# A two-layer attention kernel: its order of work rebuilt in beats of two head pairs

## The reference, cut to what matters

```
x: (64, 128, 160)   ctx: (64, 77, 256)          # 64 batch rows
# layer 0, 20 heads of 64
n = layer_norm(x);  x = x + attention(n, n)      # self, keys 128
n = layer_norm(x);  x = x + attention(n, ctx)    # cross, keys 77
h = layer_norm(x) @ w1 + b1;  a, gate = split(h) # 160 -> 2 * 640
x = x + (a * gelu(gate)) @ w2 + b2
# layer 1, 20 heads of 8
q = x @ W_q;  text keys/values from ctx[:, :73], image keys/values from ctx[:, 73:]
probs_t = softmax(q k_t / sqrt(8));  text_out = probs_t v_t
qsem = l2norm(probs_t @ ctx_text);  sem = qsem . l2norm(ctx_ip)
probs_ip = softmax(q k_ip / sqrt(8) + 0.5 sem) * spatial_mask
out = (text_out + probs_ip v_ip) @ W_out + b_out + x
```

## Time and profile before

| | |
|---|---|
| median of two runs | 3803.65 us |
| span of the profiled execution | 3799.1 us |
| TensorE busy | 3608.9 us, 95% |
| VectorE busy | 2547.7 us, 67% |
| ScalarE busy | 2592.4 us, 68% |
| GpSimd busy | 1352.4 us, 36% |
| mean granted TensorE clock | 0.995 |

### The profile page before, as it was taken

How to read it: one execution, slowest core, us unless ns; L and a number is a source line. 1 busy time by engine, 2 the same in 40 slices (tenths; PEclk the granted TensorE clock), 3 DMA queues, 4 the chain that set the end, 5 groups by cost and what they waited for, 6 DMA issues and landing times.

```text
span 3799.1 us, 88944 instructions
## 1 busy us (share of the span) xinstructions
PE 3608.9 (95%) x29708; PEld 3328.8 (88%) x29708; DVE 2547.7 (67%) x8159; ACT 2592.4 (68%) x8021; POOL 1352.4 (36%) x1658
## 2 busy tenths in 40 slices
PE   6999999999999999999999999999999999999997
PEld 5888989889898898988989899898988989889897
DVE  6667666676766666676676766767667676666766
ACT  6667676766767667676676766767676676766764
POOL 2233343333433334333333433334333343333433
PEclk9999999999999999999999999999999999999998
DMA  6522314223142321413223132231422313232130
GB/s 169 163 64 75 103 44 119 60 85 91 41 122 58 96 77 51 123 47 106 70 60 117 45 112 65 76 103 44 121 57 87 90 41 121 58 96 77 53 93 18
DMA packets 210716, 313.38 MB, mean 82 GB/s; under 512 B 31232, under 2 KB 167520, under 8 KB 210272
## 3 DMA queue, kind: packets, MB, share of 16 engines
q1 hardware_dynamic: 209984, 307.53, 27.6%
q10 hardware_dynamic: 288, 0.16, 0.0%
HBM read 267.97 MB, written 14.42 MB: 74 GB/s over the span
## 4 chain that ended last, share of the span: by engine, by line
PE 60%; DVE 17%; ACT 11%; issue 8%; POOL 4%; DMA 1%; SPq 0%; ACTq 0%; DVEq 0%; POOLq 0%
PE PS L818 8%; PE PT L840 6%; PE PV L854 6%; PE PW L798 5%; PE PG L659 5%; ACT SE L989 4%; PE PG L651 4%; PE PG L634 4%; PE PV L864 3%; DVE sums L1233 3%; PE PG L637 3%; PE PG L635 3%; PE PG L636 3%; POOL SE L1404 3%; PE PG L742 2%
## 5 line engine op out<-in xcount | busy, mean ns | idle before, releaser
L1404 POOL TENSOR_TENSOR SE<-SE,rs 128x512 f32<-128x512 f32 (+1 forms) x640 | 557.6, 871 | 1761.8 <-DVE rs L1238 1761.8
L989 ACT ACTIVATE SE<-PS,mx 128x128 f32<-128x128 f32 (+2 forms) x3840 | 982.6, 346 | 240.7 <-DVE qq L1262 128.5
L975 ACT ACTIVATE PTs<-PT 128x512 f32<-128x512 f32 (+2 forms) x960 | 575.4, 599 | 87.1 <-PE PT L840 67.9
L840 PE MATMUL PT<-ident,SE 128*128 128x128 f32 (+2 forms) x3840 | 582.0, 274 | 36.4 <-POOL SE L1404 34.6
L1233 DVE TENSOR_REDUCE sums<-SE 128x4 f32<-128x512 f32 (+1 forms) x640 | 367.0, 573 | 337.8 <-ACT SE L989 336.9
L1222 DVE TENSOR_REDUCE mx<-PS 128x4 f32<-128x512 f32 (+2 forms) x960 | 504.4, 525 | 72.1 <-PE PS L818 58.7
L840 PEld LDWEIGHTS PT<-ident,SE 128*128 128x128 f32 (+2 forms) x3840 | 465.5, 144 | 64.5 <-POOL SE L1404 49.0
L1396 POOL TENSOR_TENSOR n<-qq,p_half 128x4 f32<-128x4 f32 x320 | 345.3, 1079 | 490.2 <-DVE qq L1262 490.1
L798 PE MATMUL PW<-w_o,OTs 128*128 128x160 f32 x2560 | 415.3, 299 | 1.1 <-ACT OTs L967 1.1
L818 PE MATMUL PS<-qk 128*128 128x256 f32 x1280 | 348.5, 395 | 47.6 <-ACT qk L915 47.6
L912 ACT ACTIVATE qk<-PG 128x256 f32<-128x256 f32 x640 | 252.9, 395 | 190.1 <-PE PG L637 186.5
(11 more groups left out here) (207 smaller groups left out, 7828.5 us busy)
## 6 DMA issues: line engine op xcount, KB each, us to landing
q_slice<-q_split SPq DMA_DIRECT2D x630, 192.0 KB, 2.4
vc_slice<-vc_split SPq DMA_DIRECT2D x155, 512.0 KB, 3.6
kc_slice<-kc_split SPq DMA_DIRECT2D x150, 256.0 KB, 2.7
q1st<-q_hi SPq DMA_DIRECT2D x320, 32.0 KB, 1.9
k1st<-k_hi SPq DMA_DIRECT2D x160, 38.5 KB, 1.9
xres<-in_x_dram SPq DMA_DIRECT2D x32, 160.0 KB, 2.3
q1st<-q_lo SPq DMA_DIRECT2D x160, 32.0 KB, 1.9
out_dram<-x SPq DMA_DIRECT2D x64, 80.0 KB, 1.6
```

The costliest lines, as they stand in the source:

```text
L840: last = tr(PT[0:J, 128 * i:128 * i + 128], SE[:, place % 4, J * i:J * i + J], ident[:, :])
L975: a_(PTs[0:J, place % 3, :], PT[0:J, :], ACT.Copy).then_inc(S["pts_done"], 1)
L989: last = a_(SE[:, place % 4, J * i:J * i + J], PS[place % 2][:, step * i:step * i + J], ACT.Exp, bias=mx[:, place % 2, i:i + 1])
L1404: gp.tensor_tensor(e, e, rs[:, n % 2, :].unsqueeze(2).to_broadcast([128, 4, J]), ALU.mult)\
```

## The change

The slots are grouped in beats of three, 20 beats a group, and the unit of layer 0 becomes the duo: two head pairs (units 2d and 2d + 1). In a beat the queues hold:

- slot 0: scores of duo beat + 1, transposes of duo beat, products of duo beat - 1, the qk job of the first unit of duo beat + 2
- slot 1: the second qk job, the job "v", transposes and then scores of one unit of layer 1, and single jobs
- slot 2: single jobs, then the output projection of duo beat - 1 (both units), then the product of the unit of layer 1

Scores are four matmuls a unit instead of two: each reads 64 rows, one head, and the two heads go to the two banks of PS. Their weights and keys are the halves of qk without the zeros. Transposes are eight of 64 rows a unit instead of four of 128, the two row halves into the two banks of PT. Maximum, PT copy and OT copy are one instruction a duo. PS, PT and PV hold one duo each (before, two units in PS and in PV), and layer 1 shares PT and PV, with probabilities in tiles of its own (SE1, PTs1). The qk copy is one instruction, with the scale put into the weights' splits. The keys of cross attention are one VectorE copy into kx. x1 and cT get two sets. The norm's statistics stand in slot t, norm_out in t + 2 and xT in t + 3. The ff jobs stand in slots 51, 52, 53, 53, 54 and 66, 67, 68, 68, 69 instead of five in 56 and five in 68. keep_busy is gone.

```diff
-    STEP = 60
-    L1_SLOT = [6, 7, 9, 10, 11, 13, 14, 15, 17, 18, 22, 26, 27, 29, 33, 36, 38, 45, 49, 53]
-    NORM_SLOT = {(0, 0): -12, (0, 1): -2, (1, 0): 25, (1, 1): 40, (2, 0): 52, (2, 1): 65, (3, 0): 60, (3, 1): 71}
-    FF_SLOT = [56, 56, 56, 56, 56, 68, 68, 68, 68, 68]
+    BEATS = 20
+    STEP = 3 * BEATS
+    DUOS = NL0 // 2
+    NORM_SLOT = {(0, 0): -16, (0, 1): -1, (1, 0): 17, (1, 1): 32, (2, 0): 47, (2, 1): 62, (3, 0): 56, (3, 1): 71}
+    FF_SLOT = [51, 52, 53, 53, 54, 66, 67, 68, 68, 69]
+    DOWN_SLOT = [55, 70]
...
+                def scores(g, d):
+                    q = DUOS * g + d
+                    J, h = K0[2 * d // U0], 2 * d // NP % 2
+                    if q > 0:
+                        pe.wait_ge(S["exp_done"], 2 * q)
+                    for n in (2 * d, 2 * d + 1):
...
                         for b in range(HB):
+                            for e in range(2):
+                                rows, at = slice(DH * e, DH * e + DH), J * (2 * (n % 2) + b)
+                                last = mm(PS[:, e, at:at + J], qk[rows, n % 2, 0, 128 * b:128 * b + 128],
+                                          keys[rows, J * b:J * b + J], start=True, stop=True)
...
+                def probs_transposed(g, d):
+                    q, J = DUOS * g + d, K0[2 * d // U0]
+                    if q > 0:
+                        pe.wait_ge(S["pts_done"], q)
+                    if scored1[0]:
+                        pe.wait_ge(S["exp1_done"], scored1[0])
+                    if turned1[0]:
+                        pe.wait_ge(S["pts1_done"], turned1[0])
+                    for n in (2 * d, 2 * d + 1):
                         pe.wait_ge(S["p_done"], NL0 * g + n + 1)
+                        for i in range(4):
+                            for r in range(2):
+                                rows, at = slice(64 * r, 64 * r + 64), 64 * (4 * (n % 2) + i)
+                                last = tr(PT[0:J, r, at:at + 64], SE[rows, n % 4, J * i:J * i + J], ident[rows, rows])
```

TensorE's queue, slot by slot:

```diff
                 for t in range(FIRST, LAST):
+                    beat, part = divmod(t, 3)
+                    if part == 0:
+                        if duo_at(beat + 1):
+                            scores(*duo_at(beat + 1))
+                        if duo_at(beat):
+                            probs_transposed(*duo_at(beat))
+                        if duo_at(beat - 1):
+                            probs_v(*duo_at(beat - 1))
                     for name in qk_at(t):
                         job(name)
...
+                    if part == 1 and l1_at(beat - 1):
+                        probs_transposed1(*l1_at(beat - 1), turned)
+                    if part == 1 and l1_at(beat):
+                        scores1(*l1_at(beat), turned)
                     for name in late_at(t):
                         if name[0] != "v":
                             job(name)
+                    if part == 2 and duo_at(beat - 1):
+                        wo(g, 2 * d)
+                        wo(g, 2 * d + 1)
+                    if part == 2 and l1_at(beat - 1):
+                        probs_v1(*l1_at(beat - 1), multiplied)
```

ScalarE's queue:

```diff
+                    if sub == 0 and l1_at(beat - 1):
+                        exp1(*l1_at(beat - 1))
+                    if sub == 0 and duo_at(beat):
+                        pt_out(*duo_at(beat))
+                    if sub < 2 and duo_at(beat + 1):
+                        exp(g, 2 * d + sub)
                     for name in qk_at(t):
                         job(name)
+                    if sub == 0 and duo_at(beat - 1):
+                        ot_out(*duo_at(beat - 1))
+                    if sub == 1 and l1_at(beat - 1):
+                        pt1_out(*l1_at(beat - 1))
```

VectorE's queue, behind softmax_in in slot 0 and prob_sums(2d), "kc" and "v" in slot 1:

```diff
+                    if sub == 1 and duo_at(beat + 1):
+                        prob_sums(g, 2 * d + 1)
+                    if sub == 2 and l1_at(beat):
+                        softmax1_in(*l1_at(beat))
+                    if sub == 2 and l1_at(beat - 1):
+                        unit_out(*l1_at(beat - 1))
...
-                    for g, k, h in norms_at(t - 1):
+                    for g, k, h in norms_at(t - 2):
                         if k < 3:
                             norm_out(g, k, h)
```

More of the change, by code:

```diff
@@ L404, in xattn_program @@
                            for g in range(GROUPS) for h in range(2) for w in range(W1)]
-                          + [(STEP * g + K1_SLOT[1] + 1 + w, ("k1", g, 1, w)) for g in range(GROUPS) for w in range(W1)])
+                          + [(STEP * g + K1_STACK + w, ("k1", g, 1, w)) for g in range(GROUPS) for w in range(W1)])
         late_at = slots(
-            [(t, ("v", u[1], u[2] // 2)) for t, u in UNIT_AT.items() if u[0] == "l0" and u[2] % 2 == 0]
-            + [(t + (1 if k == 3 else 2), ("xT", g, k, h)) for t, g, k, h in NORMS]
@@ L416, in xattn_program @@
             + [(STEP * g + K1_SLOT[r], ("k1", g, r)) for g in range(GROUPS) for r in range(2)]
             + [(STEP * g + VIP_SLOT, ("vip", g, 0)) for g in range(GROUPS)]
-            + [(ctx1_slot(g, b), ("ctx1", g, b)) for g in range(GROUPS) for b in range(GB)])
+            + [(STEP * g + CTX1_SLOT[b], ("ctx1", g, b)) for g in range(GROUPS) for b in range(GB)])
         def qk_at(t):
-            if l0_at(t + 2) is None:
+            duo = duo_at(t // 3 + 2)
+            if t % 3 == 2 or duo is None:
@@ L422, in qk_at @@
                 return []
-            g, n = l0_at(t + 2)[1:]
+            g, n = duo[0], 2 * duo[1] + t % 3
             return [("qk", g, n)] + ([("kc", g, n - U0)] if U0 <= n < U0 + NP else [])
@@ new lines, in probs_v @@
+                def probs_v(g, d):
+                    q, J = DUOS * g + d, K0[2 * d // U0]
+                    pe.wait_ge(S["pts_done"], q + 1)
+                    pe.wait_ge(S["v_done"], q + 1)
+                    if q > 0:
+                        pe.wait_ge(S["ots_done"], q)
+                    if product1[0]:
+                        pe.wait_ge(S["on_done"], product1[0])
+                    for u in range(2):
+                        for b in range(HB):
+                            for e in range(2):
+                                at = 128 * (2 * e + b)
+                                last = mm(PV[DH * e:DH * e + DH, HT * u + 128 * b:HT * u + 128 * b + 128],
+                                          v_sb[0:J, d % 2, b, 2 * u + e, :], PTs[0:J, q % 2, u, at:at + 128],
+                                          start=True, stop=True)
+                    last.then_inc(S["pv_done"], 1)
@@ new lines, in probs_v1 @@
+                def probs_v1(g, k, multiplied):
+                    b, w, j = k // W1, k % W1, l1_count(g, k)
+                    pe.wait_ge(S["pts1_done"], j)
+                    if multiplied:
+                        pe.wait_ge(S["ots_done"], multiplied)
+                    if j > 1:
+                        pe.wait_ge(S["on_done"], j - 1)
+                    if w == 0:
+                        pe.wait_ge(S["gv_done"], NTH[("ctx1", g, b)])
+                        pe.wait_ge(S["gram_done"], NTH[("ctx1", g, b)])
+                    for i in range(4):
+                        off = D1 * (i % 2)
+                        last = mm(PV[:, GV * i + off:GV * i + off + GS + D1], PTs1[0:TT, 128 * i:128 * i + 128],
+                                  gv[:, b % 2, 2 * w + i // 2, off:off + GS + D1], start=True, stop=True)
+                    last.then_inc(S["pv1_done"], 1)
+                    product1[0] = j
@@ new lines, in exp1 @@
+                def exp1(g, k):
+                    j = l1_count(g, k)
+                    act.wait_ge(S["mx1_done"], j)
+                    act.wait_ge(S["sip_in"], j)
+                    if j > 2:
+                        act.wait_ge(S["qq_done"], j - 2)
+                    for i in range(4):
+                        last = a_(SE1[:, j % 2, TT * i:TT * i + TT], PT[:, 1, T * i:T * i + TT], ACT.Exp,
+                                  bias=mx1[:, j % 2, i:i + 1])
+                    last.then_inc(S["exp1_done"], 1)
@@ L997, in context_squares @@
                         act.wait_ge(S["c_dve"], HB * (2 * g + h))
+                    if g > 0:
+                        for w in range(W1):
+                            act.wait_ge(S[f"k1_in{w}"], 16 * 3 * g)
                     for b in range(HB):
```

501 lines of the change are left out of this document (216 added, 285 removed).

## The result

The changed kernel takes 4837.26 us (median of two runs, 4829.09 and 4845.43) against 3803.65, 1.271 times as long, with a 95% interval of 1.2685 to 1.274. The forecast was 3853, in a range of 3620 to 4080: 984 us too low, with the result outside its range.

A forecast was written before the change was run, and what follows sets the result against it. TensorE's queue was taken to bound the kernel, busy 95% of the span. Head 240, 15 groups of 233.9 (work -11.8, waits +14.2), tail 100 and 4.6 around the span gave 3853 us, range 3620 to 4080.

The forecast's parts named there:

- TensorE's work: Scores, transposes and changes of tile in a group: -8.4 - 1.6 - 3.2 + 1.4 = -11.8 us.
- rival 2: Scores and half transposes of every beat: row halves do not run side by side; 4190 us, chance 0.15.
- self transposes: Probabilities' transposes in self units: 128-column loads keep four paired steps at 0.11 us, so nothing saved.
- the middle: TensorE's added waits a group, taken between 0 and the net 28.3 us: 14.2 us.
- full price: All TensorE waits of the new order in a group: 36.6 us, or 28.3 net of today's 8.3 idle.
- xT: Transposes in the third slot wait for norm_out: 7.8 us a group in self beats, 3.5 in cross beats.
- GELU beats: Table loads and gelus lengthen ScalarE's loop to 16.0 us; TensorE loses 3.6 and 1.0, twice: 9.2 a group.
- norm_stats ahead of the maximum: VectorE's statistics delay the next maximum, which has 0.3 us to spare: about 1.2 in four of six, 4.9 a group.
- My loop: Self beat with one set of PS, PT, PV: 9.0 us against TensorE's 8.6, losing 1.6 a group.
- The single product on its PT copy: Layer 1's product waiting for its PT copy, named among TensorE's longest waits; no separate size given.
- a tail over 120: Sign in the kernel's tail, forecast at 100 us: above 120, the clock there is what was missed.
- Rival 3: Steady groups with the forecast's waits at full price: 248.0 us a group, 4065 us; no separate chance.

The follow-up runs named there:

- all four edits: Changed kernel with norm_out and context_scale a slot earlier, output projection before single jobs, ff jobs in slots 52/67, tail jobs at 6, 7, 9, 10: 4075.64 us.
- the last kernel: all four edits, plus matmuls for nothing in 12 waits of a group and ten in each beat of the tail: 3991.44 us.

## Why the prediction was wrong, point by point

**TensorE's work: right in sum, in part by luck.** -11.8 us a group was forecast, which with the 8.3 idle taken off is 211.4 of work; found 209.5, or 211.0 with the idle time at the lower clock taken out. Added up by kind, from start to next start without idle time and with passes at the lower clock halved, a group has (before, after): scores of layer 0 26.0 and 19.5 us, transposes of both layers' probabilities 26.3 and 19.3, products of layer 0 21.8 and 20.4, all else 148.7 and 151.8. So the transposes saved 7.0 where 3.2 were booked, scores and products with their changes of tile 7.9 where 8.6 were, and the rest, booked at nothing, cost 3.1. Row halves run side by side; TensorE's timeline of the changed kernel, a cross duo at full clock:

```profile
2000.63 1.12 PE L775 MATMUL PS<-kx,qk 64*128 64x77 f32 x16
2001.64 0.77 PE L793 MATMUL PT<-ident,SE 64*77 64x64 f32 x16
```

Sixteen scores in 1.01 us to the next line, change of tile included, where 2 us would have been rival 2. The rule of the Trainium skill ("TensorE: Matmul & The Clock Gate", Part 3: Packing small matmuls), that a load overlaps a pass in flight only in another row group, did not become this kernel's limit. The term furthest off was the self transposes: nothing was booked, and 0.59 us for sixteen halves against 1.02 for eight whole ones saves some 3 to 4 us a group of ten self duos.

**The waits: the kind right, the size wrong, and this is the step that failed first.** "Lateness is shared ... I take the middle, 14.2": with today's 8.3 that is 22.5 us idle a group. Measured 57.6, so 35 us a group or 526 us. The middle had no row behind it. The full price, 36.6, was nearer and still short, by 21. The named places were the right ones: xT (11.3 at full price, 18.6 measured), cT (4.8, 6.6), oT1 (4.8, 4.5), GELU beats (9.2, 8.5 on the product alone). Of six xT waits in a group three lie in self beats, 3.37 us each on average for 2.6 booked, and three in cross beats, 2.52 for 1.2; so the cross price was the worse one. In self beats norm_out takes 2.35 us, not 1.82, and in the beat shown GpSimd works beside it. The lower clock is not a reason: the self waits were 3.3 to 3.4 us in all beats but one (3.8), at a mean clock from 0.70 to 1.00. The maximum starts 3.45 us after its scores in the beat shown and in the one at full clock alike; the scores end at 2138.61 in the one shown and VectorE comes to the maximum at 2139.98, behind the norm's statistics. What had no term at all is the group on the qk copy, 15.4 us in the changed kernel. An extra job in slot 0 (ipT, y) or ahead of v takes one of two job banks, so the next job needs the copy of the first qk one job sooner. My loop counted that copy among the links of ScalarE and never asked which bank it frees. The 4.9 booked for norm_stats ahead of the maximum belongs to this group too: on top of all four edits, moving them behind the maximum took 9.8 us a group off v's waits for the copy, and put them at the transposes. The single product on its PT copy, named as one of the longest waits, has 6.2 us in the whole kernel.

**The clock: missing.** The prediction spoke of it for the tail only. In the steady groups it cost 26.3 us by the halves (395 us in all), and filling the waits made a group 20 shorter. The evidence was there: before the change a stretch of the tail with 3.2 us idle in 20 stood at 0.81, and the steady stretch with 8.3 in 230 at 1.00. My forecast moved the steady part towards the first, to 22.5 idle in 234, and kept the clock of the second. The Trainium skill ("TensorE: Matmul & The Clock Gate", A second HAM failure mode: psum-queue depth-cycling) tells of another kernel in which frequent short idle times between groups of matmuls make the clock swing between its two levels. The trace agrees: in the fifteen groups no wait is longer than 3.8 us, and 52.6 us of 293.4 run at 1.2 GHz.

**Head, tail, surroundings.** Head 284.0 for 240 (+44) and tail 141.8 for 100 (+42), for the same two reasons. The head has 81.0 us idle at clock 0.89, where the kernel before had 43.5 at 0.99; the tail has 43.5 idle at 0.57, where it had 20.0 at 0.88. The prediction's sign for a missed clock, a tail over 120, came true, but in the last kernel fillers brought the tail's clock to 0.84 and only 12 us of it back, so the clock is not the whole of it. The median lies 10.0 over the profiled span where 4.6 was booked: 1.8 lie around the span of that execution (4829.09 less 4827.3), and 8.2 are the distance from it to the median. With 15 x 35.1, 15 x 26.3 and 15 x -1.9 these make the 984: 526 + 395 - 28 + 44 + 42 + 5.

**Table loads: right in number.** ScalarE's loads in the changed kernel (count, busy us, mean ns):

```profile
L922 ACT ACT_TABLE_LOAD x95 | 121.9, 1283 | 1.7
L977 ACT ACT_TABLE_LOAD x63 | 80.8, 1283 | 1.1
L995 ACT ACT_TABLE_LOAD x31 | 39.8, 1283 | 0.6
```

189 here and 192 forecast. Putting the jobs together gained 83 us where the forecast's term of 9.2 a group had said up to 147.

**Rival 3** (full price, 4065) missed by 772 us, since it too left out the clock and the bank. The chance of 0.39 for slower by over 2% was too low: the rows that made the third slot's inputs late spoke for it, and the half price held it down.

What stays open is the rule by which idle time becomes lower clock. Whole transposes and GELU jobs together both had less idle time than the changed kernel and more time at the lower clock (69.1 and 59.8 against 52.6). Idle time causes it, as the fillers show, but its sum does not set its size. Where in a beat the idle time falls, or what work stands around it, may matter; no run here tells. Open too is what bounds the new order at 245.5 us a group: a second set of PS, PT or PV was not tried.

## What to carry to other kernels

When a forecast says that an engine that was 95% busy will now wait, ask what its clock does, with the kernel's own idle stretches as the gauge; the clock here added about half as much again to the idle time. Price a late input at its full length and look for ready work behind it in the same queue: moving that work ahead of it is one edit (351 us here), and making the input a slot earlier is another (572 us). Where several jobs share two banks, follow each bank from its writer to its reader for every slot that holds an extra job, since a wait taken from one job comes back at the next one.

## What the runs showed of the hardware that was not expected

- Matmuls that compute nothing made the kernel faster by 229 us (160 a group, 4837 to 4608), though no input was made earlier.
- One instruction of norm_out on 128x128 took 0.34 us alone, and two took 1.01 and 0.78 us while GpSimd multiplied from 2146.00 to 2147.77. Made a slot earlier, the same two instructions had means of 0.43 and 0.34 us for 0.48 and 0.57 in the changed kernel. The Trainium skill ("SBUF — State Buffer", Who interferes with whom) says that a VectorE instruction with two inputs in SBUF contends with a GpSimd instruction that reads SBUF; the trace agrees.
- Half transposes of 64 rows in pairs step by 0.074 us (0.59 for eight pairs, change of tile behind them included), whole ones by 0.11.
- With the mean clock at 0.72 a stretch of a beat took 8.44 us where at full clock it took 8.18, because 1.60 us of the latter was idle.
